# Perceiver layer on one core: two score products instead of one ahead of the first batch's probability transposes

## The reference, cut to what matters

```
xn = layer_norm(x, g_x, b_x);  cn = layer_norm(context, g_c, b_c)
q = heads(xn @ Wq);  k = heads(cn @ Wk);  v = heads(cn @ Wv)     # 16 heads of 64
sim = einsum('bhid,bhjd->bhij', q, k) / sqrt(64)
attn = softmax(sim, axis=-1)
out = einsum('bhij,bhjd->bhid', attn, v) ... @ Wo
```

## Time and profile before

| what | value |
|---|---|
| time, median of 3 runs | 1384.32 us (1384.16 to 1385.14) |
| profiled execution, its own time | 1384.79 us |
| profiled execution, span first to last instruction | 1383.2 us |
| PE busy | 1275.2 us, 92% |
| DVE busy | 1035.3 us, 75% |
| ACT busy | 888.9 us, 64% |
| mean granted TensorE clock | 0.979 of full speed |

### The profile page before, as it was taken

One profiled execution on the slowest core, in us unless ns is written; L12 is line 12 of the kernel. 1 busy time (PEld: TensorE's weight loads), 2 busy tenths in 40 slices (PEclk: granted clock), 3 DMA queues, 4 the chain that ended last, 5 costly groups with the idle time before them and its releaser, 6 DMA issues.

```text
span 1383.2 us, 26632 instructions
## 1 busy us (share of the span) xinstructions
PE 1275.2 (92%) x8320; PEld 839.2 (61%) x8321; DVE 1035.3 (75%) x2246; ACT 888.9 (64%) x1434; POOL 223.7 (16%) x265
## 2 busy tenths in 40 slices
PE   5899999999999999999999789999999999999990
PEld 5668668687686686776866544555555555555540
DVE  5675877876877778768766668878787878787875
ACT  3577777676777766867777346666666666666650
POOL 1001003021030030210200321212121212121102
PEclk9999999999999999999999899999999999999995
DMA  9437245264262451643614992863636365611104
GB/s 363 153 112 246 85 173 193 65 245 140 105 250 84 160 204 65 230 141 114 247 70 163 355 357 63 303 232 94 232 94 232 94 230 195 204 23 23 23 9 129
DMA packets 71107, 224.77 MB, mean 163 GB/s; under 512 B 5718, under 2 KB 5956, under 8 KB 64916
## 3 DMA queue, kind: packets, MB, share of 16 engines
q1 hardware_dynamic: 64704, 210.03, 41.4%
q0 software_dynamic: 6336, 14.24, 5.0%
q10 hardware_dynamic: 28, 0.01, 0.0%
HBM read 177.78 MB, written 46.48 MB: 162 GB/s over the span
## 4 chain that ended last, share of the span: by engine, by line
PE 78%; DVE 9%; ACT 5%; issue 4%; DMA 1%; POOL 1%; DVEq 0%; ACTq 0%; POOLq 0%
PE bank L1678 9%; PE bank L1636 8%; PE bank L748 6%; PE bank L749 6%; PE bank L750 6%; PE bank L728 6%; PE bank L729 6%; PE bank L730 6%; PE bank L1599 4%; PE bank L1704 4%; PE bank L1620 3%; PE bank L738 3%; PE bank L1726 2%; PE bank L1645 2%; PE bank L1660 2%
## 5 line engine op out<-in xcount | busy, mean ns | idle before, releaser
L1636 PE MATMUL bank<-moe_w 128*128 128x257 f32 x768 | 189.8, 384 | 6.5 <-DVE moe_w L1023 6.5
L1636 PEld LDWEIGHTS bank<-moe_w 128*128 128x128 f32 x768 | 138.2, 192 | 25.7 <-DVE moe_w L1023 5.8
L728 PE MATMUL bank<-moe_w,arena 128*128 (+1 forms) x368 | 139.5, 379 | 0.7 <-DVE arena L591 0.7
L729 PE MATMUL bank<-moe_w,arena 128*128 (+1 forms) x368 | 139.5, 379 | 0.0
L730 PE MATMUL bank<-moe_w,arena 128*128 (+1 forms) x368 | 139.5, 379 | 0.0
L1678 PE MATMUL bank<-moe_w 128*128 128x512 f16 x384 | 114.4, 379 | 10.0 <-ACT moe_w L1080 7.0
L476 ACT ACTIVATE wosT<-moe_w,now_v_act 128x1024 f16 (+1 forms) x92 | 100.7, 1142 | 27.1 <-PE bank L750 27.1
L1066 ACT ACTIVATE moe_w<-bank,cols,ugain 128x512 f32<-128x512 f32 x96 | 74.6, 777 | 61.6 <-PE bank L1679 60.7
L546 DVE SCALAR_TENSOR_TENSOR arena<-bank,now_b,arena 128x512 f32<-128x512 f32 x92 | 69.0, 750 | 52.2 <-PE bank L730 48.1
L1285 DVE TENSOR_TENSOR moe_w<-bank,moe_w 128x512 f16<-128x512 f32 (+1 forms) x96 | 65.4, 689 | 48.3 <-ACT moe_w L1080 46.1
L421 POOL DMA_INDIRECT acc_rows<-arena,job_idx x23 | 36.7, 1597 | 393.7 <-DVE arena L623 393.7
(11 more groups left out here) (270 smaller groups left out, 3067.7 us busy)
## 6 DMA issues: line engine op xcount, KB each, us to landing
moe_w<-in_L_ffn_w_dram SPq DMA_DIRECT2D x46, 1024.0 KB, 6.2
moe_w<-w_halves SPq DMA_DIRECT2D x8, 4096.0 KB
moe_w<-in_L_ffn_w_dram SPq DMA_DIRECT2D x8, 4096.0 KB
w_halves<-moe_w SPq DMA_DIRECT2D x48, 512.0 KB, 3.7
arena<-in_ctx_dram SPq DMA_DIRECT2D x32, 384.0 KB
arena<-in_L_ffn_w_dram SPq DMA_DIRECT2D x10, 1024.0 KB, 4.9
blocks<-in_L_ffn_w_dram SPq DMA_DIRECT2D x8, 1024.0 KB, 4.8
arena<-in_L_ffn_b_dram SPq DMA_DIRECT2D x8, 1024.0 KB
```

The source lines that it names most:

```text
L728: nc.tensor.matmul(bank[fb % 2][:, :], xT_low[:, k, :], high, start=(k == 0), stop=False)
L729: nc.tensor.matmul(bank[fb % 2][:, :], xT_high[:, k, :], high, start=False, stop=False)
L1636: last = nc.tensor.matmul(bank[h][:, 0:KEYS], qkT[:, c, b, h * P:(h + 1) * P], cnT[:, b % 2, c, :], start=(c == 0), stop=(c == KC - 1))
```

## The change

On PE, in the turn b = 1 alone, each of the three `pt_fill(g, 0, k)` moves one place back: `scores(g, 1, 0)`, `scores(g, 1, 1)`, `pt_fill 0`, `scores(g, 1, 2)`, `pt_fill 1`, `scores(g, 1, 3)`, `pt_fill 2`. Before, they stood behind the scores 0, 1 and 2. On DVE, in the same turn, each `pt_lo(g, 0, k)` moves one place back likewise: `row_max 0`, `pt_lo 0`, `row_max 1`, `pt_lo 1`, `row_max 2`, `pt_lo 2`, `row_max 3`. ACT's order stays as it is, and so do the turns b = 2 and 3 and every transfer. At L524 the lower bound of one tile is applied to all eight experts and not to the first alone: one instruction over 8 elements a row, where it was 1.

```
@@ moe_dve
-            link(nc.vector.tensor_scalar(tiles[:, 0:1], tiles[:, 0:1], 1.0, None, ALU.max))
+            link(nc.vector.tensor_scalar(tiles[:, :], tiles[:, :], 1.0, None, ALU.max))
@@ body of DVE
                     for k in range(HG):
                         if do_a:
-                            if b >= 1 and k < 3:
-                                pt_lo(g, b - 1, k)
+                            part = k - 1 if b == 1 else k
+                            if b >= 1 and 0 <= part < 3:
+                                pt_lo(g, b - 1, part)
                             row_max(g, b, k)
@@ body of PE
-                        if do_a and b >= 1 and h < 3:
-                            pt_fill(g, b - 1, h)
+                        part = h - 1 if b == 1 else h
+                        if do_a and b >= 1 and 0 <= part < 3:
+                            pt_fill(g, b - 1, part)
```

## The result

| | before | after |
|---|---|---|
| time, median of 5 | 1384.16 us (1384.15 to 1385.14) | 1395.52 us (1393.57 to 1399.97) |
| profiled execution, its own time | 1384.79 us | 1395.40 us |
| its span | 1383.2 us | 1393.8 us |
| mean granted TensorE clock | 0.979 | 0.974 |

The ratio is 1.0082, with a 95% interval of 1.007 to 1.0093: slower by 11.4 us, where 3.7 were forecast, and above the range of 1384.0 to 1392.0 us. The single times of the changed kernel spread by 6.4 us. Those of the kernel before spread by 1.0 us here, but by 3.7 to 6.4 us on the three later occasions, with 15 to 29 runs.

A forecast was written before the change was run, and what follows sets the result against it. PE was taken as busiest (92%), with DVE's list setting the end of turn 1. Groups 1 to 7 at 2.3 us plus group 0 at 1.4 us gave 3.7 us: 1388.0 us, range 1384.0 to 1392.0 us.

The forecast's parts named there:

- The gap that goes: PE, turn 1, groups 1 to 7: the 0.76 us gap ahead of `pt_fill 0` disappears, filled by a second score product.
- What is late next: Groups 1 to 7: `row_max 0` delays DVE's `pt_lo 0`, and so `pt_fill 2`, by 0.33 us; PE waits 0.4 us there.
- The cover that goes: Groups 1 to 7: scores 3 no longer cover the 2.12 us chain from `pt_fill 2` to `ct_fill`; PE idles about 1.5 us.
- Group 0: Turn 1 of group 0: lower clock costs 1.8 us, earlier `ct_fill` returns 0.38 us; 1.4 us later (1.1 to 2.3).
- Tile count: L524 over eight elements: 0.02 us, or 0.1 us at several times that; taken as 0, with numbers and jobs unchanged.
- the clock falls in groups 1 to 7 too: Rival: gaps of 0.4 and 1.5 us lower PE's clock, about 1.6 us a fall; 1389.6 to 1399 us; chance 0.13.
- DVE's term: Groups 1 to 7: `row_max` ahead of `pt_lo 0` on DVE, 7 x 0.33 = 2.3 us (0 to 2.9).
- Only DVE's term: Rival: no added clock cost in group 0; seven groups +2.3 us, group 0 -0.4 us: 1386.2 us; chance 0.21.
- the larger half of the falls: Upper part of the rival with one to seven clock falls, 1389.6 to 1399 us; left out of the range.

The follow-up runs named there:

- filling groups 1 to 7 alone: The changed kernel, unread products in PE's turn 1 gaps of groups 1 to 7, group 0 left open: 1391.93 us, +6.7 us over the kernel before.
- filling all: The changed kernel, unread products in PE's turn 1 gaps of every group, group 0 included: 1387.78 us, +2.7 us over the kernel before.

## Why the prediction was wrong

Its direction was right, and so was the replay of the places; the size was not: 3.7 us for 11.4.

- *The gap that goes*: right. No wait ahead of `pt_fill 0` in the seven groups, and nothing gained by it.
- *What is late next*: the mechanism was right, its term too small. `row_max` ahead of `pt_lo 0` takes 0.45 us, not 0.33. I had read its cost from a `row_max` that starts under the tail of a `pt_lo`; behind `heads_apart` it starts after the end, and the next one waits for its end too. My upper bound, the whole duration of 0.42, was also too low. 7 x 0.45 = 3.2 us for 2.3, confirmed by DVE's half alone (+3.0). That the short gap came out at 0.39 us where I had written 0.4 is luck: my 0.4 counts from start to start. In the measure of the brackets (scores 3 end at 422.62 + 1.47 = 424.09) my replay has 0.26 us, and the longer `row_max` made 0.39 of it.
- *The cover that goes*: right to 0.01 us as a chain (2.12), and PE is idle for 1.47 us. The step that failed is what I said of its price. I counted this gap at nothing in groups 1 to 7 and put the fall of the clock there among the rivals, at 0.13. "Against it: from 458 to 460 us PE was busy for 0.83 us of 2 and the clock stayed at 1.00" is true of one gap. The change makes two, 0.39 and 1.47 us with 0.65 us of work between, and the profiles show that it takes both: with the short one filled or absent, no fall in 14 places. In place of the 0 stand three falls of 1.57 us in each of the two profiles, 4.7 us. The price for a fall, about 1.6 us, was right.
- *Group 0*: the 1.4 us were nearly right for the profiled execution, where its `o_proj` starts 58.43 us after its first scores and started 56.96 after them before, 1.47 us more. That is partly luck, since it hangs on which executions are compared: group 0 takes 94.17, 95.35, 95.21 and 95.14 us in the four profiles with the changed order and its gaps there, and 92.90 and 92.32 us in the two with the order of before, once with a fall in turn 1 and once without. So the term is 1.3 to 3.0 us. Over the runs, filling groups 1 to 7 alone leaves 4.0 us more than filling all. Part of that is the wait for a transfer at group 0's end, which I had not looked at.
- *Tile count*: right.
- *Rivals*: "the clock falls in groups 1 to 7 too" came true, with its three falls and its price: 1388.0 + 3 x 1.6 = 1392.8, and with the 0.9 us that DVE's term was short 1393.7. The rest up to 1395.5 fits what group 0 can cost beyond my 1.4 us, but no run separates it. "Only DVE's term" leaned on the Trainium skill, "TensorE: Matmul & The Clock Gate", section "Why this matters for your kernels", which asks for no idle gaps above about 3 us between bursts of matmuls. By it the clock would have stayed up. The traces disagree again: it fell behind 0.39 and 1.47 us.

My range left out "the larger half of the falls" on the ground of one row. In the same trace stood two pairs of gaps with a fall. At the end of group 0 a gap of 1.53 us comes shortly behind one of 0.78, and the 32 products behind it take 8.83 us. The changed kernel's trace has the same pair there without a fall, and they take 7.14 us; of all 13 traces, 7 have this fall.

```profile
103.83 0.63 PE L1712 MATMUL bank<-ident,arena 128*128 128x128 f32 x4 [0.78 <-DVE arena L1224]
105.98 8.83 PE L1704 MATMUL bank<-moe_w 128*128 128x256 f32 x32 [1.53 <-ACT moe_w L1053]
```

The other pair is that of the earlier trace rows, which I misread as a fall with a second gap behind it. The work between its gaps (764.64 to 765.30) ran at full speed, and the clock fell only in the second gap, at about 765.4:

```profile
764.00:765.00 1.00, 0.36 (x3) 0.36 (x4) 0.90 (x8) 1.00 (x3) 0.01 (x1) 1.00 0.84 305
765.00:766.00 1.00, 0.30 (x3) 0.06 (x1) 0.86 (x6) 1.00 (x2) 0.00 (x0) 0.69 0.98 352
```

Both rows were of the kind that the change makes, and I used neither for groups 1 to 7.

## What to carry to other kernels

Before work is moved ahead of a wait, ask which engine the next wait ends on: here DVE's list, not PE's, released the bank, and the move only took the cover from the next chain. Price new idle time on TensorE by the clock as well as by its length, and look for gaps that stand close together: 0.4 us of waiting in front of a 1.5 us gap cost 1.6 us in 6 of 14 places. One trace that shows no fall behind a gap doesn't settle it, since the next execution may fall there. To take time out, move the task that stands in the releasing engine's list.

## What the runs showed of the hardware that was not expected

- Two gaps of PE together, 0.39 and 1.47 us, were followed by the lower clock in 3 of 7 groups in each of two profiles; the long gap alone (1.39 to 1.47 us) in none of 14.
- No length of a gap decides alone. At group 0's end a single gap of 1.83 to 2.07 us, behind some 17 us without another, was followed by a fall in 5 of 5 traces, and one of 1.63 us was not. In group 0's turn 1 the transposes right behind a gap of 2.61 to 2.94 us ran at the lower clock (1.07 to 1.12 us) in 3 of 8 traces and at full speed (0.65 us) in the others.
- The groups with a fall differ from one execution of the same program to the next (2, 4, 6 and 3, 5, 7).
- A row maximum (128x257 out of an accumulation bank, 0.42 us long) holds DVE for 0.33 us behind a `pt_lo` and for 0.45 us behind the copies of `heads_apart`, with a `pt_lo` next both times: the step depends on what stood ahead of it.
